# Attention in eight steps per tile with four heads in row groups of TensorE; two pairs of banks for the turned scores, one for the plain ones

## The reference, cut to what matters

```python
def _L0_xattn_ref(x, c, Wq, bq, Wk, bk, Wv, bv, Wo, bo):
    h = N_HEADS                                   # 8
    kc = ch // h                                  # 8
    d_rope = int(kc * 0.5)
    q = _proj(Wq, bq, x)
    k = _proj(Wk, bk, c)
    v = _proj(Wv, bv, c)
    ...
    q = _rope(q, d_rope)
    k = _rope(k, d_rope)
    scores = jnp.einsum('bhqd,bhkd->bhqk', q, k) / jnp.sqrt(jnp.float32(kc))
    p_attn = jax.nn.softmax(scores, axis=-1)
    out = jnp.einsum('bhqk,bhkd->bhqd', p_attn, v)
    ...
    return _proj(Wo, bo, out)

x = x + jnp.tanh(g_xattn[0]) * _L0_xattn_ref(_layernorm(x, axis=-1), ctx_2048, ...)
```

## Time and profile before

| | us |
|---|---|
| median of 3 runs | 1577.44 |
| lowest and highest | 1573.41, 1581.14 |
| the profiled execution | 1564.62 |
| its span, first to last instruction | 1562.6 |
| mean granted TensorE clock in it | 0.958 |
| TensorE matmuls busy in the span | 1451.1 |
| VectorE, ScalarE, GpSimd busy | 953.7, 775.4, 535.0 |

### The profile page before, as it was taken

One profiled execution on the slowest core, in us unless ns is written; L12 is line 12 of the kernel. 1 busy time (PEld: TensorE's weight loads), 2 busy tenths in 40 slices (PEclk: granted clock), 3 DMA queues, 4 the chain that ended last, 5 costly groups with the idle time before them and its releaser, 6 DMA issues. The chain is left out here.

```text
span 1562.6 us, 32056 instructions
## 1 busy us (share of the span) xinstructions
PE 1451.1 (93%) x10096; PEld 1209.4 (77%) x10097; DVE 953.7 (61%) x1817; ACT 775.4 (50%) x1425; POOL 535.0 (34%) x592
## 2 busy tenths in 40 slices
PE   3999999999999986999988999999978699999998
PEld 2777777777777755888877888888867478888887
DVE  7888887888788734776655433333324466666653
ACT  4466666666666663333223333333332656666652
POOL 4332332332333201744455443320005344455220
PEclk9999999999999995999999999999995799999999
DMA  5122122112212202211265332221125001111000
GB/s 176 57 57 62 53 55 62 54 53 62 55 52 62 54 3 77 105 41 55 71 196 190 121 94 91 91 67 54 50 57 175 27 28 41 42 42 41 15 14 28
DMA packets 89081, 106.54 MB, mean 68 GB/s; under 512 B 12208, under 2 KB 80432, under 8 KB 88368
## 3 DMA queue, kind: packets, MB, share of 16 engines
q1 hardware_dynamic: 79264, 73.60, 15.9%
q0 software_dynamic: 9744, 31.99, 6.4%
HBM read 54.29 MB, written 25.03 MB: 51 GB/s over the span
## 5 line engine op out<-in xcount | busy, mean ns | idle before, releaser
L422 ACT ACTIVATE e_t<-st_ps 128x512 f32<-128x512 f32 x512 | 277.9, 595 | 165.7 <-PE st_ps L527 165.2
L369 DVE TENSOR_REDUCE row_max<-s_ps 128x4 f32<-128x1024 f32 x256 | 311.0, 1217 | 32.5 <-PE s_ps L510 32.4
L510 PE MATMUL s_ps<-k_st,q_st 96*128 96x256 f32 x1024 | 196.7, 315 | 13.0 <-DMA q_st<-q_part 11.7
L527 PE MATMUL st_ps<-q_st,k_st 104*128 104x256 f32 x1024 | 170.2, 287 | 1.6 <-ACT e_t L422 1.5
L510 PEld LDWEIGHTS s_ps<-k_st,q_st 96*128 96x128 f32 x1024 | 147.4, 193 | 21.9 <-DMA q_st<-q_part 12.5
L527 PEld LDWEIGHTS st_ps<-q_st,k_st 104*128 104x128 f32 x1024 | 143.6, 189 | 6.6 <-ACT e_t L422 5.2
L546 PE MATMUL o_ps<-e_t,v_st 128*32 128x256 f32 x2048 | 137.0, 385 | 0.9 <-ACT e_t L422 0.9
L1599 POOL DMA_INDIRECT gathered_tail<-sorted_results,result_at x64 | 70.1, 1095 | 153.7 <-POOLq L2090 135.4
L1457 PE MATMUL y_ps_moe<-w_all_moe,xt_hi_moe 128*128 x568 | 113.3, 283 | 3.8 <-DVE xt_lo_moe L1276 3.8
L1836 DVE TENSOR_TENSOR h_all_tail<-silu_tail,u_ps_tail 128x512 f32<-128x512 f32 x64 | 43.9, 685 | 115.5 <-ACT silu_tail L1707 65.1
L1282 DVE TENSOR_TENSOR h_all_moe<-silu_moe,u_ps_moe 128x512 f32<-128x512 f32 x71 | 48.8, 687 | 107.2 <-PE u_ps_moe L1435 107.2
(11 more groups left out here) (310 smaller groups left out, 3592.6 us busy)
## 6 DMA issues: line engine op xcount, KB each, us to landing
k_st<-k_part SPq DMA_DIRECT2D x384, 32.0 KB
q_st<-q_part SPq DMA_DIRECT2D x96, 128.0 KB, 3.2
stage_moe<-in_experts POOLq DMA_DIRECT2D x21, 512.0 KB, 4.3
rows_in_moe<-sorted_rows SPq DMA_DIRECT2D x71, 128.0 KB, 2.0
sorted_results<-y_sb_moe SPq DMA_DIRECT2D x71, 128.0 KB
c_in<-in_ctx SPq DMA_DIRECT2D x33, 128.0 KB, 2.1
xn_moe<-in_ctx SPq DMA_DIRECT2D x8, 512.0 KB
context_tail<-in_ctx SPq DMA_DIRECT2D x8, 512.0 KB, 10.9
```

The source lines that it names most:

```text
L369: nc.vector.tensor_reduce(out, s_ps[s_ // 2 % 2][:].rearrange("p (j h) t -> p j h t", j=2), AX_X, ALU.max).then_inc(s["max_taken"], 1)
L422: nc.scalar.activation(e_t[h % 8][:], st_ps[h % 2][:], ACT.Exp, scale=float(DH) ** -0.5)\
L510: last = nc.tensor.matmul(s_ps[s_ // 2 % 2][:, 2 * (h - s_) + half_, :], q_st[r][0:ROWS, u, half_ * P:(half_ + 1) * P], k_st[r][0:ROWS, u, ...
L527: last = nc.tensor.matmul(st_ps[h % 2][:, half_, :], k_st[r][0:MROWS, u, j, half_ * P:(half_ + 1) * P], q_st[r][0:MROWS, u, :], start=True ...
```

## The change

The heads of a unit lie in the four groups of 32 rows of `q_st` and `k_st`: in each group, row 4c+t holds part t of channel c, and every fourth row is free; two of these (`MAX_ROWS`, eight rows in all) hold the maxima, against ones in `k_st`. `k_st` shrinks from 16 to 4 planes, without zeroed copies. A score matmul reads 32 rows. A body has 8 steps `p`; a step makes the plain scores of two heads and the turned scores of two others, in two rounds of four matmuls, each in its own row group. Plain scores have one pair of banks, turned ones two pairs; the exponential takes two heads at once; the value product goes by halves of a unit in every step.

The users of `misc` come in another order: keys (step 0), maxima (1), queries (2), second turn of tile n-2 (3), turned results (4), y (5), values (6), turned results (7). Rotation is one product; its bias is computed once (`turned_bias`) and added by GpSimd; the value bias goes into the output bias. GpSimd normalises x. The value copy moves to ScalarE. The mixture of experts and what follows are not touched.

```diff
-    LAG = 8
-    ROWS, MROWS = 96, 104
+    STEPS = HP // 2
+    LAG = 5
+    MAX_ROWS = slice(3, P, 16)
...
-        k_st = [sb(f"k_st{r}", [P, UNITS, UH, D], F32R) for r in range(RING)]
+        k_st = [sb(f"k_st{r}", [P, UNITS, D], F32R) for r in range(RING)]
...
-        s_ps = [ps(f"s_ps{r}", [P, 4, D]) for r in range(2)]
-        st_ps = [ps(f"st_ps{r}", [P, 2, D]) for r in range(2)]
+        s_ps = ps("s_ps", [P, 2, 2, D])
+        st_ps = [ps(f"st_ps{r}", [P, 2, 2, D]) for r in range(2)]
...
                     sp.wait_ge(s["k_high"], n + 3)
...
+                    for t in range(2):
+                        sp.dma_start(k_st[r][t:P:4, :, :].bitcast(F32), part["k"][:, 0, :].bitcast(F32))\
+                            .then_inc(k_stacked[r], 16)
...
+                    sp.wait_ge(s["q_high"], n + 3)
+                    for t in (0, 2):
+                        sp.dma_start(q_st[r][t:P:4, :, :].bitcast(F32), part["q"][:, 0, :].bitcast(F32))\
+                            .then_inc(q_stacked[r], 16)
                     sp.wait_ge(s["q_split"], n + 3)
...
+                    sp.dma_start(q_st[r][1:P:4, :, :].bitcast(F32), part["q"][:, 1, :].bitcast(F32))\
+                        .then_inc(q_stacked[r], 16)
...
+            def parts_of(a, n, c, i):
+                r, before = (c + 2) % RING, (c + 1) % RING
+                pool.wait_ge(s[a + "_roped"], n + 3)
+                nc.gpsimd.tensor_tensor(bare[a][:], roped[a][:, 0, :], roped[a][:, 1, :], ALU.add)\
+                    .then_inc(s[a + "_summed"], 1)
+                pool.wait_ge(s[a + "_summed"], n + 3)
+                nc.gpsimd.tensor_tensor(whole[a][:], bare[a][:], turned_bias[a][:], ALU.add).then_inc(s[a + "_whole"], 1)
...
             def body(n, c, i):
                 if there(n, c, 2):
...
+                    parts_of("k", n, c, i)
                 if there(n, c, -2):
                     pool.wait_ge(s["y_taken"], n - 1)
...
+                    row = x_row(n - 2)
+                    nc.gpsimd.tensor_tensor(row, row, like_row(n, y_sb), ALU.add).then_inc(s["y_free"], 1)
+                if there(n, c, 2):
+                    parts_of("q", n, c, i)
+                if there(n, c, 3):
+                    normalize(n, 3)
...
+                nc.vector.tensor_tensor(roped[a][:].rearrange("p a t -> p (a t)"), misc[:],
+                                        rope[:].rearrange("p a t -> p (a t)"), ALU.mult).then_inc(s[a + "_roped"], 1)
...
+                for p in range(STEPS):
+                    if p == 0 and there(n, c, 0):
+                        split_max(n, c)
+                    if there(n, c, 1):
+                        take_max(n, c, p)
+                    if p == 0 and there(n, c, 2):
+                        rope_parts("k", n, c)
+                    if p == 2 and there(n, c, 2):
+                        rope_parts("q", n, c)
+                    if p == 4 and there(n, c, -1):
+                        normalize_out(n, 0)
+                    if p == 5 and there(n, c, 3):
+                        stats_of(n, 3)
+                    if p == 7 and there(n, c, -1):
+                        normalize_out(n, 1)
...
+                    if p == 5 and there(n, c, -2):
                         act.wait_ge(s["y_projected"], n - 1)
                         act.wait_ge(s["y_free"], n - 1)
                         nc.scalar.activation(y_sb[:], misc[:, 0:D], ACT.Identity, bias=out_bias[:],
                                              scale=tanh_gain[:, 0:1]).then_inc(s["y_taken"], 1)
...
+            def score_step(n, c, i, p):
+                k, t = later(p, LAG)
+                turned = list(scores_turned(c, k, t)) if there(n, c, k) else []
+                plain = list(scores(c, p)) if there(n, c, 1) else []
+                if turned:
+                    if t == 0:
+                        pe.wait_ge(m_stacked[(c + k) % RING], 16 * uses(c, i, k))
+                    wait_count(pe, s["exp_done"], STEPS * (n + k) + t - 1)
+                    wait_alone(pe)
+                if plain:
+                    if p == 0:
+                        pe.wait_ge(q_stacked[(c + 1) % RING], 64 * uses(c, i, 1))
+                        pe.wait_ge(k_stacked[(c + 1) % RING], 48 * uses(c, i, 1))
...
+                    wait_count(pe, s["max_taken"], (n + 1) * STEPS + p)
+                for at in range(0, 4, 2):
+                    for of, done in ((turned, "st_scored"), (plain, "scored")):
+                        for out, w, moving in of[at:at + 2]:
+                            last = nc.tensor.matmul(out, w, moving, start=True, stop=True)
+                        if of and at == 2:
+                            last.then_inc(s[done], 1)
...
+                    score_step(n, c, i, p)
+                    use_values(n, c, p)
...
+                    if p == 5 and there(n, c, -2):
+                        pe.wait_ge(s["a_taken"], n - 1)
+                        if there(n, c, -1):
+                            pe.wait_ge(s["o_normed"], 2 * (n - 1) + 1)
+                        nc.tensor.matmul(misc[:, 0:D], w_out[:], a_t[:], start=True, stop=True)\
+                            .then_inc(s["y_projected"], 1)
```

More of the change, by code:

```diff
@@ L205, in body @@
[L205 to L212, removed]
@@ L223, in body @@
-                    sp.wait_ge(s["q_split"], n + 3)
[L224 to L229, removed]
+                    sp.dma_start(k_st[r][2:P:4, :, :].bitcast(F32), part["k"][:, 1, :].bitcast(F32))\
+                        .then_inc(k_stacked[r], 16)
@@ L254, in body @@
[L254 to L267, removed]
-                        nc.gpsimd.tensor_copy(part[a][:, 0, :], whole[a][:]).then_inc(s[a + "_high"], 1)
-                        pool.wait_ge(s[a + "_high"], n + 3)
-                        nc.gpsimd.tensor_tensor(part[a][:, 1, :], whole[a][:], part[a][:, 0, :].bitcast(F32),
-                                                ALU.subtract).then_inc(s[a + "_split"], 1)
@@ L435, in project, with scores @@
                 last.then_inc(s[a + "_projected"], 1)
-            def body(n, c, i):
-                for s_ in range(HP):
-                    if s_ == 0 and there(n, c, -2):
-                        pe.wait_ge(s["a_taken"], n - 1)
-                        nc.tensor.matmul(misc[:, 0:D], w_out[:], a_t[:], start=True, stop=True)\
-                            .then_inc(s["y_projected"], 1)
-                    if s_ == 2 and there(n, c, 2):
-                        if isinstance(n, int) and n < 2:
+            def scores(c, p):
+                r = (c + 1) % RING
+                for half_ in range(2):
+                    for at in range(2):
+                        u, j = (2 * p + at) // UH, (2 * p + at) % UH
+                        rows = slice(32 * j, 32 * j + 32)
+                        yield (s_ps[:, at, half_, :], q_st[r][rows, u, half_ * P:(half_ + 1) * P],
+                               k_st[r][rows, u, :])
@@ new lines, in use_values @@
+            def use_values(n, c, p):
+                k, t = later(p, LAG + 2)
+                if there(n, c, k):
+                    r, u, half_ = (c + k) % RING, t // 2, t % 2
+                    if half_ == 0:
+                        pe.wait_ge(s["exp_done"], STEPS * (n + k) + 2 * u + 2)
+                        if u == 0:
+                            pe.wait_ge(s["v_stored"], n + k + 1)
+                        if u % 2 == 0:
+                            wait_count(pe, s["o_taken"], 2 * (n + k) + u // 2)
+                    for j in range(UH):
+                        last = nc.tensor.matmul(o_ps[32 * j:32 * j + 32, u % 2, :], v_st[r][:, half_, u * UH + j, :],
+                                                e_t[(2 * u + j // 2) % 4][:, j % 2, half_, :],
+                                                start=(half_ == 0), stop=(half_ == 1))
+                    last.then_inc(s["pv_done"], 1)
@@ L470, in body @@
+                    if p == 6 and there(n, c, 2):
+                        if there(n, c, -2):
+                            pe.wait_ge(s["y_taken"], n - 1)
+                        elif there(n, c, -1):
+                            pe.wait_ge(s["o_normed"], 2 * (n - 1) + 1)
+                        else:
+                            pe.wait_ge(s["q_roped"], n + 3)
                         for h in range(2):
@@ L552, in _, with value_bias @@
-            steps(pe, body)
+                        pe.wait_ge(s["o_normed"], 2 * (n - 1) + 1)
+                        pe.wait_ge(s["o_taken"], 2 * n)
+                        turn_out(1)
+            def value_bias():
+                pe.wait_ge(more_consts_in, 3 * 16)
+                pe.wait_ge(s["v_stored"], 1)
+                nc.tensor.matmul(misc[:, 0:1], w_out[:], bias[:, 5:6], start=True, stop=True)\
+                    .then_inc(s["value_bias_made"], 1)
+            steps(pe, body, None, value_bias)
```

435 lines of the change are left out of this document (202 added, 233 removed).

## The result

| | before | after |
|---|---|---|
| median of 4 runs each, us | 1575.43 | 1687.18 |
| lowest and highest | 1572.04, 1581.14 | 1685.52, 1689.78 |
| profiled execution | 1564.62 | 1689.78 |
| its span | 1562.6 | 1688.0 |
| mean granted TensorE clock | 0.958 | 0.907 |

A forecast was written before the change was run, and what follows sets the result against it. TensorE bounds the old kernel; the new one stalls on queries, period 21.3 against 16.9 us. 28 bodies give +123, ends -1: profiled 1564.6 + 122 = 1687, plus 12.8 to the median, 1700 us; range 1640 to 1820.

The forecast's parts named there:

- The query chain: GpSimd's queries queue behind the residual add waiting for y of step 5; next tile's scores wait, TensorE idle 4.8 us.
- Scores of a step: Eight 32-row score matmuls on TensorE, two rounds in four row groups side by side: 0.57 us; one after another 1.25.
- The column groups: Value product's four matmuls in four column groups span 0.42 us against 0.385 for one; nearest evidence for row groups.
- Bank loop: Single bank pair for plain scores: maximum 1.22, hand-over 0.03, scores 0.57, at least 1.82 us a step; rival's chance 5%.
- Clock: TensorE's pause brings 1.2 GHz; a cold step 0 adds 1.45 us, entered as +1.0 a tile on the mean.
- Landing: Last of three query DMAs on SP lands 3.4 us after its issue starts, at 20.2 in the tile.
- From y to GpSimd: Hand-over to GpSimd's residual add after y's ScalarE pass: 0.08 us; y starts 1.07 us after step 5 begins.
- The ends: Start-up, bodies -1 to 1 (15 to 16 us as now) and the last four bodies: -1 us together.
- The sum: 28 bodies x (21.3 - 16.9) = +123 us, ends -1: +122 us on the profiled execution, giving 1687.
- The Trainium skill's rule on loads: Round two's weights load only after round one streams: some 0.1 us a step, under 1 us a tile; left out.
- The drain on a change of mode: TensorE drains at three tiling mode changes a step: at most about 0.3 us a tile, 8 us in all.
- the walk: One new tile traced through steps 0 to 7 from old durations: about 15.7 us without the query chain.

The follow-up runs named there:

- the kernel with the add last: New kernel with GpSimd's residual add moved behind the queries' split: 1543.25 us, ratio 0.979 to the kernel before.
- the spare sum: One extra 256-wide GpSimd sum ahead of the queries' sum: 1710.25 us in the new kernel, 1548.44 us in the kernel with the add last.
- the unharmed kernel before: Kernel before with only GpSimd's order changed to keys, residual add, queries, y staying in step 0 of 16: 1578.76 us, ratio 1.001.

## Why the prediction was right, and where its numbers were off

- **The query chain.** Right in every link, and shown by the moved add, by the spare sum (on the path in one kernel, off it in the other) and by the unharmed kernel before.
- **Scores of a step.** 0.57 taken, 0.59 measured. The column groups were the right neighbour of the unknown.
- **Bank loop.** 1.82 a step taken; 1.86 measured (416.99 to 418.85 and to 420.71). Without the chain 15.7 taken, 15.64 measured (the kernel with the add last).
- **Clock.** The pause does bring the lower clock, in 27 of 28 bodies. From step 0 to step 5 11.6 us were taken for a cold body, and 11.83 measured (405.16 to 416.99). The term entered as +1.0, a mean; measured +1.68. This was mis-sized low, by counting a doubt about frequency as if it were a share of bodies.
- **Landing.** 3.4 us taken, 2.3 measured (402.87 to 405.16). This is the mis-sized term on the other side, -1.1. The six DMAs of the earlier trace rows had the keys' DMAs queued close around them; in the new order the queries are alone. That the neighbours made the difference is argued only. With it the pause is 3.4 and not 4.8 us, nor the 4 or more that was named as a sign, and the period 20.5 instead of 21.3.
- **From y to GpSimd.** 0.08 taken, 0.19 measured; y itself starts 1.00 after step 5 instead of 1.07. The bias sum, cast and issues came as costed (2.15 against 2.16).
- **The ends.** -1 taken, about +7.5 measured. The prediction had bodies -1 to 1 at 15 to 16 us as before; by their key projections they took 18.2, 19.4 and 16.7, where the kernel before took 14.6, 16.6 and 16.9, so the start-up lost 5.5 us. The query chain has no part in it: with the add last body 2 projects its keys at 79.1 us, no earlier. It is the bank loop at the lower clock, which the prediction reckoned only at full clock. TensorE waits 1.32 us for the maximum, its four matmuls then span 0.80 us instead of 0.50, and a step takes 2.12 us; with two pairs for the plain scores body 2 projects its keys at 68.2. The last bodies cost some 2.0 more. One such step:

```profile
35.51 0.80 PE L498 MATMUL s_ps<-k_st,q_st 32*128 32x256 f32 x4 [1.32 <-DVE row_max L361]
```

- **The sum.** 28 x 3.57 = 100 instead of 123, +7.5 instead of -1: 107.5 against 122. That the total came within 13 us is in part luck: the clock (+0.7 us a tile) and the ends (+8.5 us) were taken too low, the landing (1.1 us a tile) too high.
- **The Trainium skill's rule on loads.** By the Trainium skill, page "TensorE: Matmul & The Clock Gate", section on packing small matmuls, the second round of weights would wait for the first round of the same row group. The trace does not agree: weights of the second round load from 400.19 while the first round's matmuls, from 400.08 to 400.47, are still running by the profile (their ends are modelled), and eight scores are read after 0.59 us, not after the 0.67 that the prediction's estimate for the rule, 0.1 more, would give. The sum rightly left it out. The other half of what the prediction quoted, starts of different row groups some 4 ns apart, agrees: the four matmuls of a round start at 400.08 and 400.09.
- **The drain on a change of mode.** The Trainium skill, page "TensorEngine Tiling (Array Packing)", key properties, has TensorE drain when the tiling mode changes. The trace agrees: at full clock the weight loads sit idle 0.41 us behind a value product, as before (417.99 us, for one). It cost nothing beyond the walk.

## What to carry to other kernels

When a producer is moved to a later step, look up every engine that waits for it in program order, and what stands behind that wait: here an add whose result nobody needed soon held up the one piece of work the next tile waited for, at 4.8 us in each tile. A wait in the middle of an in-order queue is harmless only as long as its event comes first, so put work for the far end of the pipeline last. And price a pause twice: its length, and what the engine runs at afterwards (here half as much again).

## What was not expected of the hardware

- TensorE stayed at its lower level of 1.2 GHz for nearly the whole attention, at 99% busy, when all score matmuls used one row group of 32 (clock 0.53 over 400 to 600 us); with two groups, at 91% busy, it ran at 2.4 GHz (clock 1.00 over 400 to 500 us). Each is one run, and what in the work made the difference is open.
- Forty-eight short matmuls a body, where the later version had 13 long ones, cost little in three bodies of four and some 7 us in the fourth, where the loop turns; instruction packets rose from 48 to 97.
- Matmuls of free row groups started ahead of earlier ones whose groups were busy (402.64 before 402.85), so the order within a step, by twos or by fours, was of next to no account: the scores came 0.60 against 0.59 us after the first.
